# A three-layer transformer kernel: last resident loads moved ahead of the third layer, row sums given a bank of their own, first masked scores placed ahead of the reciprocals on VectorE

## What is computed

```
x = x + attention(LN1(x))            with mask_a        (phase A)
x = x + attention(LN2(x), ctx)       with mask_b        (phase B)
x = x + gelu(LN3(x) @ w1) @ w2                          (MLP)
a = LN(ctx);  Q = x @ Wq.T;  K = a @ Wk.T;  V = a @ Wv.T
x = x + tanh(gate) * softmax(Q K.T * scale, masked with -inf by mask_d) V @ Wo.T   (phase D)
```

## Time and profile before

| | |
|---|---|
| time, median of 3 runs | 1099.28 us (1098.64 to 1102.71) |
| profiled execution: its own time | 1102.0 us |
| profiled execution: span of the instructions | 1100.3 us |
| PE busy | 1070.6 us (97%) |
| DVE busy | 825.2 us (75%) |
| ACT busy | 704.2 us (64%) |
| POOL busy | 482.8 us (44%) |
| mean granted clock of TensorE | 0.995 |

### The profile page before, as it was taken

How to read it: one execution, slowest core, us unless ns; L and a number is a source line. 1 busy time by engine, 2 the same in 40 slices (tenths; PEclk the granted TensorE clock), 3 DMA queues, 4 the chain that set the end, 5 groups by cost and what they waited for, 6 DMA issues and landing times.

```text
span 1100.3 us, 24221 instructions
## 1 busy us (share of the span) xinstructions
PE 1070.6 (97%) x8741; PEld 928.6 (84%) x8741; DVE 825.2 (75%) x1299; ACT 704.2 (64%) x2354; POOL 482.8 (44%) x361
## 2 busy tenths in 40 slices
PE   7989999999999999999999999999999998999998
PEld 7888888888888888887898888888888987888886
DVE  6678787778888888878878667667787466777767
ACT  4678777777788788786444534544545375666676
POOL 3675666567777677666513122113122232222210
PEclk9999999999999999999999999999999998999999
DMA  6366665577776777654253142251748256666621
GB/s 216 108 188 206 196 199 175 183 222 221 221 230 211 226 218 223 183 181 133 83 145 106 64 156 84 90 172 34 234 132 293 94 183 200 209 211 208 194 69 59
DMA packets 145832, 185.92 MB, mean 169 GB/s; under 512 B 17857, under 2 KB 88753, under 8 KB 145713
## 3 DMA queue, kind: packets, MB, share of 16 engines
q1 hardware_dynamic: 145712, 184.37, 53.3%
HBM read 122.59 MB, written 61.73 MB: 168 GB/s over the span
## 4 chain that ended last, share of the span: by engine, by line
PE 48%; DVE 16%; ACT 13%; issue 7%; POOL 6%; DMA 4%; SPq 2%; DVEq 0%; ACTq 0%; POOLq 0%
PE psum L1081 15%; PE psum L1062 14%; PE psum L887 8%; POOL prob L2196 6%; ACT prob_blocks L1366 4%; DVE prob L1746 3%; ACT prob L1366 3%; PE psum L1001 3%; PE psum L879 3%; DVE negmax L1759 2%; ACT second_prob_blocks L1366 2%; ACT inputs_transposed L1404 2%; DVE ln_tile L1681 2%; DVE inputs_transposed L1688 1%; PE psum L923 1%
## 5 line engine op out<-in xcount | busy, mean ns | idle before, releaser
L887 PE MATMUL psum<-inputs_hi,weights_hi 128*128 128x256 f32 x768 | 223.9, 292 | 4.8 <-POOL inputs_lo L2182 2.5
L887 PE MATMUL psum<-inputs_lo,weights_hi 128*128 128x256 f32 x768 | 217.5, 283 | 0.0
L887 PE MATMUL psum<-inputs_hi,weights_lo 128*128 128x256 f32 x768 | 217.3, 283 | 0.0
L2196 POOL TENSOR_TENSOR prob<-prob,mask_bias 128x1024 f32<-128x1024 f32 x64 | 152.7, 2408 | 101.3 <-DVE prob L1746 99.3
L887 PEld LDWEIGHTS psum<-inputs_hi,weights_hi 128*128 128x128 f32 x768 | 147.0, 191 | 10.2 <-issue 4.3
L1759 DVE TENSOR_REDUCE negmax<-prob 128x8 f32<-128x1024 f32 x96 | 115.7, 1212 | 50.0 <-POOL prob L2196 50.0
L1366 ACT ACTIVATE prob<-prob,negmax 128x128 f32<-128x128 f32 x384 | 148.3, 392 | 0.5 <-DVE negmax L1759 0.5
L887 PEld LDWEIGHTS psum<-inputs_lo,weights_hi 128*128 128x128 f32 x768 | 147.3, 192 | 0.2
L887 PEld LDWEIGHTS psum<-inputs_hi,weights_lo 128*128 128x128 f32 x768 | 147.2, 192 | 0.0
L2182 POOL TENSOR_TENSOR inputs_lo<-inputs_transposed,inputs_hi 128x512 fp32r<-128x512 f32 x70 | 93.6, 1358 | 94.4 <-DVE inputs_hi L1719 61.6
L1366 ACT ACTIVATE prob_blocks<-prob,negmax 128x128 f32<-128x128 f32 x304 | 117.5, 389 | 18.0 <-DVE negmax L1759 17.6
(11 more groups left out here) (132 smaller groups left out, 2665.5 us busy)
## 6 DMA issues: line engine op xcount, KB each, us to landing
prob_turned<-prob_blocks SPq DMA_DIRECT2D x38, 512.0 KB, 3.0
prob<-prob_turned SPq DMA_DIRECT2D x152, 128.0 KB, 3.4
weights_whole<-weights_in SPq DMA_DIRECT2D x72, 256.0 KB, 3.2
inputs_transposed<-normalised SPq DMA_DIRECT2D x120, 128.0 KB, 2.9
normalised<-ln_tile SPq DMA_DIRECT2D x24, 512.0 KB, 2.8
context<-row_sums_spread SPq DMA_DIRECT2D x188, 64.0 KB, 2.1
stream<-residual SPq DMA_DIRECT2D x42, 256.0 KB, 2.9
ln_tile<-stream SPq DMA_DIRECT2D x32, 256.0 KB, 3.9
```

Of the source, the lines that this page charges most:

```text
L887: mm = pe.matmul(ps[:, bank, GT * part:GT * part + GT], w[:, slot, c, o], a[:, buf, c, :], start=c == 0 and i == 0, stop=c == KC - 1 and i ...
L2196: pool.tensor_tensor(half, half, mb.unsqueeze(1).to_broadcast([128, 8, T]), ALU.add).then_inc(s_biased, 1)
```

## The change

Four edits, all in phase D.

1. SP issues `load_inputs(3)` and `load_stream_tiles(3)` before the first step of D, behind the inputs of that step.
2. For a `WHOLE` item both halves of the product with V go to bank 4 (`value_bank`), in different columns. Bank 5 is left to the row sums. `context` waits for the whole product.
3. PE's `row_sums(g)` waits, where `g` and `g - 1` are both `WHOLE`, for the copy of the row sums before (`s_rc`) and no longer for `context(g - 1)`.
4. In the ten steps 34 to 43, DVE makes the mask bias and the first half of the masked scores of `g` before the reciprocals of `g - 1`, the turning of its second blocks and the context of `g - 2`.

```diff
+        def value_bank(g, half):
+            return T_BANK if g in WHOLE else T_BANK + half
...
-                if g == 33:
-                    load_inputs(3)
-                    load_stream_tiles(3)
...
             load_mask(D, 0)
             load_transposed(STEPS[D][0].fill)
+            load_inputs(3)
+            load_stream_tiles(3)
             for st in STEPS[D]:
                 step(st)
...
                 if g in WHOLE:
-                    pe.wait_ge(s_cx, 2 * g)
+                    if g - 1 in WHOLE:
+                        pe.wait_ge(s_rc, g)
+                    else:
+                        pe.wait_ge(s_cx, 2 * g)
...
-                        out = ps[32 * j:32 * j + 32, T_BANK + c // 2, T * c:T * c + T]
+                        out = ps[32 * j:32 * j + 32, value_bank(g, c // 2), T * c:T * c + T]
...
-                dve.wait_ge(s_pv, 4 * g + 2 * h + 2)
+                dve.wait_ge(s_pv, 4 * g + (4 if g in WHOLE else 2 * h + 2))
                 dve.wait_ge(s_rsp, 64 * (g + 1))
...
                 if g - 1 in WHOLE:
+                    make_mask_bias(g)
+                    mask_scores(g, 0)
                     inverse_sums(g - 1)
                     turn_second_blocks(g - 1)
                 if st.ends and not late:
                     context(g - 2, 0)
                     context(g - 2, 1)
-                if st.ends and not late and phase == D:
+                if st.ends and not late and phase == D and g - 1 not in WHOLE:
                     make_mask_bias(g)
                     mask_scores(g, 0)
```

More of the change, by code:

```diff
@@ L1785, in context @@
                 half = slice(256 * h, 256 * h + 256)
-                dve.wait_ge(s_pv, 4 * g + 2 * h + 2)
+                dve.wait_ge(s_pv, 4 * g + (4 if g in WHOLE else 2 * h + 2))
                 dve.wait_ge(s_rsp, 64 * (g + 1))
-                dve.tensor_tensor(ctxn[:, half], ps[:, T_BANK + h, half], ctxn[:, half], ALU.mult).then_inc(s_cx, 1)
+                dve.tensor_tensor(ctxn[:, half], ps[:, value_bank(g, h), half], ctxn[:, half], ALU.mult).then_inc(s_cx, 1)
             def context_lo(g, h):
```

## The result

| | median | lowest to highest | runs |
|---|---|---|---|
| kernel before, same chip | 1101.24 us | 1098.64 to 1489.15 (one outlier; the next is 1105.16) | 20 |
| changed kernel | 1103.73 us | 1100.66 to 1106.84 | 20 |

The ratio is 1.0025, with a 95% interval of 1.0016 to 1.0033. That is 2.75 us longer (0.0025 x 1101.24), within 0.5% and on the side that was forecast, +1.8. The median of the kernel before moved by 2 us from three runs to twenty, so kernels are compared by their ratios, or by medians taken beside each other. The profiled execution of the changed kernel took 1103.86 us with a span of 1102.3, against 1100.3 of span before.

What follows compares the result with a forecast made beforehand. PE was taken to bound the kernel before, the circle steps 34 to 43 after. Gains of 5.3 + 1.8 = 7.1 us against 8.9 taken back give +1.8: 1099.28 + 1.8 = 1101.1 us, 8-in-10 range 1093 to 1107.

Steps and rivals of the forecast that it cites:

- The circle: Steps 34 to 43: mask's DMA, masked scores, reciprocals, turning, SP's store and next mask form a loop, 14.8 us a turn.
- The reduction to 14.8: Turn taken below the parts' 15.02, since SP waits longer before each store and neighbouring transfers get more time to land.
- The sum: Nine turns from 896.8 put step 43's reciprocals at 1031.8; the end moves by +1.8 us.
- The first wait, 0.71 at 898.57, stays: PE's first row-sum wait for the context, before item 33, keeps its 0.71 us, as the item before isn't `WHOLE`.
- Point (1): Sign: PE's gap before item 33's product with V gone, second blocks landing 3 to 4 us after store, full clock near 900 to 930.
- PE sets the pace: Regular pair of steps in phase D: PE, busy 27.58 of 28.09 us, bounds the kernel before.
- the term of 1.8 for edits 2 and 3: PE's row-sum waits for the context in phase D, 2.5 us less the first 0.71, go: 1.8 us gained.
- The 5.26 of edit 1: Step 35, 18.21 us where 12.95 is regular: issuing the large loads sooner removes the 5.26 us.
- Points (2) and (3): Signs: DVE waits for the mask's DMA in steps 35 to 43; PE's row sums wait for reciprocals, odd products for second blocks.
- PE as the bound at 13.8 a step: Rival: a turn under 13.8 us in phase D leaves only the gains, 1092.2 us; chance 0.21.
- The longer circle: Rival: turns in steps 34 to 43 average 15.7 us, nine cost 8.1 more, 1109 us; chance 0.14.
- The loads' harm: Rival: early in D the moved loads delay step 32's inputs or item 33's mask by at most 4 us, 1105; chance 0.05.

Runs made afterwards that it cites:

- e3: Changed kernel, all four edits, with SP issuing the next mask's load ahead of the store of the second blocks in steps 33 to 43; 0.9924 of the kernel before, 1093.29 us.
- e9: Changed kernel with the mask's load moved ahead of the four DMAs that spread the row sums, still behind the store; 0.9941 of the kernel before, 1096.09 us.
- e5: Changed kernel plus an idle 128-byte DMA, waited for by SP, right before the next mask's load in steps 34 to 43; 1.0132 of the kernel before, 1115.92 us.
- e6: Changed kernel plus the same idle 128-byte DMA and wait as e5, but right behind the mask's load; 1.0000 of the kernel before, 1101.95 us.
- e4: Kernel before with only edit 4, the new order on DVE; 1.0059 of the kernel before, 1107.97 us.
- e8: Kernel before with only the mask's load moved to the head of SP's step in steps 33 to 43; 1.0007 of the kernel before, 1102.44 us.
- e2: Edits 1 to 3 on the kernel before, DVE's order as before; 0.9962 of the kernel before, 1097.25 us.
- e1: Kernel before with only edit 1, the two large loads ahead of phase D; 0.9975 of the kernel before, 1098.23 us.

## Why the prediction was right, step by step

**The circle.** Right, and shown: cut (e3), or shorter than PE's step (e9), it costs nothing, longer by 1.56 it costs 14 us (e5 against e6), alone it costs 6.5 (e4), and without edit 4 there is none to cut (e8). Its parts against those measured, means over the nine turns of the changed kernel:

| part | forecast | measured |
|---|---|---|
| mask bias to SP's store | 1.80 + 1.39 = 3.19 | 3.27 |
| store to the mask's issue | 8.49 | 8.27 |
| mask's issue to DVE | 3.34 | 3.34 |
| turn | 15.02, taken as 14.8 | 14.89 |

The reduction to 14.8 was in the right place, since the train did become shorter, but most of it came in the first five turns; from the 9.48 of step 39 on the trains took 8.19 to 9.48, around the old mean of 8.49. The first turn is not the circle's alone: its mask had landed before DVE came to it, 3.92 after the issue, and on the way to the store the scores held DVE up by 0.79.

**The sum.** The reciprocals of step 43 were to start at 1031.8 and did at 1031.90; the span moved by 2.0 where 1.8 was said, the ratio by 2.75. The start was 0.7 early (896.07 for 896.8) and the nine turns 0.8 long (134.0 for 133.2); that these two cancel is luck. The mask of step 44 was to reach DVE at 1044.9 and did at 1044.69.

**"The first wait, 0.71 at 898.57, stays".** This step was wrong. It grew to 2.25, since the context now stands behind mask 34's own wait of 2.93. The clock fell behind it, and the 24 matmuls of the projection behind it took 4.20 us (900.16 to 904.36), where at the spacing of the first ones (900.35 to 901.41 for nine, 0.12 each) they would take about 2.9. It cost the sum little, as PE was not the bound: the product with V of item 33 followed at 910.15 without a gap, the scores behind it held DVE up by 0.79, and the first turn was 15.07. Point (1) of what would show it, a full clock near 900, was therefore not met, though its other parts were (stores landed 3.0 us after 899.27). That the clock falls behind such a gap is not a given either: in e5 it stayed at 1.00 behind 2.29 us.

**"PE sets the pace" of a regular pair.** Wrong, by the chain of the kernel before and by e2: with PE's wait for the context gone the pair stayed at 28.1, so the term of 1.8 for edits 2 and 3 was not to be had in the regular steps, and the 1.0 of e2's median isn't clear of noise. PE's busy share of 27.58 in 28.09 and a chain over ScalarE and DVE that closes in the same 28.09 can't be told apart by the share. That DVE waited 1.2 to 1.7 us for ScalarE before most reciprocals was in the rows, and was read only as room for edit 4. With the circle cut, edit 4 gained 0.6 us a pair there (e3 against e2).

**The 5.26 of edit 1.** Right in kind; 4.9 in the length of D of e1 but 2.8 (1.0 to 4.5) by the ratio. It was read as the price of the late blocks alone, but the half clock behind the gap is in it, and it came from an execution with the lowest mean clock that any of the kernel before has, 0.995.

Together the two terms came to 7.1; e2, which is just these edits, gave 4.2 by its ratio (0.0038 x 1101.43), 6.65 in the traces. On top of e2, edit 4 costs 6.9 by the ratios (0.0063 x 1101) where 8.9 was said. By the ratios both sides were too large by 2 to 3 us, and that their difference came out close is luck in part; by the length of D edit 4 costs 209.8 - 201.05 = 8.75, and both sides fit. The two measures differ by 2 to 2.5 us, less than executions of one kernel do.

**Points (2) and (3).** DVE waits for the mask's DMA in nine of ten steps, 0.6 to 4.4 us, as said. PE's row sums wait for the reciprocals 1.1 us only; its idling lies before the product with V, 7.1 us, and ends with the landing of the second blocks, as forecast, though in even steps as well as in odd ones.

**The rivals.** PE as the bound at 13.8 a step is what e3 has, 27.34 to 27.56 a pair. By the rule of the Trainium skill that was weighed ("DMA: Bandwidth & Descriptors", section "Anatomy of one DMA — SWDGE (gpsimd) path") the turn would have been 12.4, an estimate; it was 14.89, and the mask took 3.34 to reach DVE. The measurement decides, and the page's figure is for another issuing path. The longer circle was near in single turns (16.12, 15.48, 15.37), not in the mean. The loads' harm was not there (e1).

## What to carry to other kernels

Before an instruction that waits for a DMA is put ahead of others, follow what those others release: if it leads through an in-order queue back to the issue of that same DMA, add up the loop's latency and compare it with the step; here 14.9 us of latency beat 13.7 us of work, with no engine full. Such a loop is cheap to cut: issuing a 16 KB load earlier in its queue turned a change of +0.25% into one of -0.76%. And an engine that is 98% busy is only shown to be the bound when taking its last wait away makes the step shorter; the chain of work, followed back from its end, could have told it here before any experiment.

## What the runs showed of the hardware

- After an idle time of 2.25 us and 1.4 us of work on PE the granted clock was 0.51 from 901.40 to 904.40, and back at 1.00 from 905. Behind the same wait of step 34 it was 0.50 for 3 us in e6 (900 to 903) and in e9 (903.50 to 906.50), but stayed at 1.00 in e5, where the gap was 2.29 us. In the kernel before it was 0.50 from 911.70 to 917.00, behind a gap of 4.44 us.
- A DMA of 128 bytes, waited for by the queue that issued it, took 1.39 to 1.69 us from issue to the next issue (e5); the 16 KB of a mask took 3.34 until DVE ran, on average of nine.
- Moving a DMA or a wait by one place in the queue costs nothing or 14 us by whether a loop runs through that place (e6, e5).
